# Other places for additions, scale factors, ranks and gates in the last fifth of a fused attention and FFN kernel

## The reference

```python
# block 1: a chosen 64x64 matrix per sequence, then attention with 4-bit weights
h = einsum('bct,bcd->bdt', x, cond_w[condition])
q, k, v = (h @ ((qw - 8) * scales) for each)       # 32 query heads, 8 key/value heads of 128
x = x + softmax(mask(rope(q) @ rope(k).T / sqrt(128))) @ v @ ((qw_o - 8) * scales_o)
# block 2: a gated two-layer map per sequence, then a dense layer with a routed low-rank part
h = gelu(einsum('bct,bch->bht', x * cmask, W_sess[ids]) + b_sess[ids])
s = (einsum('bht,hs->bst', h, W2) + b2) * tmask    # one row of 1024 per token
base = s @ W_base.T + b_base                       # 1024 -> 1024
logits = s @ W_router.T; top-2 of 8, softmax       # the gates w, one per token and expert
lora = 2 * einsum('ter,te,eor->to', s @ A, w, B)   # rank 16 for each of 8 experts
x = x + base + lora
```

## Time and profile before

| | us |
|---|---|
| median of three executions (lowest, highest) | 1913.29 (1912.41, 1917.9) |
| the profiled execution | 1915.91 |
| its span, first to last instruction | 1913.9 |
| busy in the span: TensorE matmul, VectorE, ScalarE, GpSimd | 1729.1, 1598.4, 1407.5, 61.3 |

### The profile page before, as it was taken

The page is one execution under the profiler, slowest core; times in us unless marked ns, Lnnn a source line. Parts: engine busy times, 40 slices in busy tenths (PEclk is TensorE's granted clock), DMA queues, the critical chain, the costliest instruction groups (busy, mean ns, idle before and its releaser), DMA issues. The chain is left out here.

```text
span 1913.9 us, 38885 instructions
## 1 busy us (share of the span) xinstructions
PE 1729.1 (90%) x14314; PEld 937.1 (49%) x14314; DVE 1598.4 (84%) x2715; ACT 1407.5 (74%) x2372; POOL 61.3 (3%) x50
## 2 busy tenths in 40 slices
PE   3668999998999899999999998999999978899998
PEld 3424545554554445445544554554544545455553
DVE  5589999999899898989998998899999987556642
ACT  2557988888898888888888888898888775233420
POOL 0200000000000000000000000000000011111100
PEclk8789999999999999999999999999999999899999
DMA  6321030011102010301021012102013111100001
GB/s 212 101 88 46 12 67 23 24 34 47 46 2 72 9 46 1 78 3 46 14 66 29 20 36 45 46 2 74 5 55 101 52 50 55 67 23 34 23 34 44
DMA packets 118582, 87.66 MB, mean 46 GB/s; under 512 B 11996, under 2 KB 110692, under 8 KB 118372
## 3 DMA queue, kind: packets, MB, share of 16 engines
q1 hardware_dynamic: 117732, 84.76, 14.9%
q10 hardware_dynamic: 640, 0.13, 0.0%
HBM read 76.49 MB, written 8.39 MB: 44 GB/s over the span
## 5 line engine op out<-in xcount | busy, mean ns | idle before, releaser
L1311 ACT ACTIVATE pj<-pj,ratio 128x512 f32<-128x512 f32 x865 | 575.4, 684 | 120.0 <-PE pj L1645 114.6
L1643 PE MATMUL pj<-hid,wts 128*128 128x512 f16 x1024 | 392.8, 384 | 66.8 <-DVE pj L826 25.0
L1645 PE MATMUL pj<-hid,wts 128*128 128x512 f16 x1024 | 390.9, 382 | 0.0
L1320 ACT ACTIVATE sbk<-sbk,wts 128x512 f32<-128x512 f32 x384 | 261.8, 682 | 24.2 <-PE sbk L1712 18.9
L1320 ACT ACTIVATE sa<-sa,wts 128x512 f32<-128x512 f32 x384 | 260.8, 679 | 15.6 <-PE sa L1712 15.5
L1643 PEld LDWEIGHTS pj<-hid,wts 128*128 128x128 f16 x1024 | 99.8, 97 | 235.8 <-ACT pj L1311 71.3
L1655 PEld LDWEIGHTS tp<-wts,hid 128*128 128x128 f16 x3072 | 181.7, 98 | 32.5 <-issue 3.5
L1655 PE MATMUL tp<-wts,hid 128*128 128x128 f16 x3072 | 192.5, 219 | 0.5
L1645 PEld LDWEIGHTS pj<-hid,wts 128*128 128x128 f16 x1024 | 100.7, 98 | 77.3 <-issue 1.4
L726 DVE SCALAR_TENSOR_TENSOR work<-pj,ratio,cos_t 128x512 f32<-128x512 f32 x128 | 95.7, 748 | 44.5 <-PE pj L1645 35.5
L1311 ACT ACTIVATE ex<-ex,ratio 128x512 f32<-128x512 f32 x193 | 127.9, 663 | 4.1 <-PE ex L1645 1.6
(11 more groups left out here) (247 smaller groups left out, 3090.4 us busy)
## 6 DMA issues: line engine op xcount, KB each, us to landing
wts<-qo_d SPq DMA_DIRECT2D x64, 256.0 KB, 3.2
y<-x_d SPq DMA_DIRECT2D x7, 2048.0 KB, 7.8
wts<-qq_d SPq DMA_DIRECT2D x35, 256.0 KB, 3.2
int_even<-qq_d SPq DMA_DIRECT2D x29, 256.0 KB, 3.0
out_d<-y SPq DMA_DIRECT2D x12, 512.0 KB, 2.6
work<-qv_d SPq DMA_DIRECT2D x16, 256.0 KB, 7.7
work<-sv_d SPq DMA_DIRECT2D x16, 256.0 KB, 9.4
work<-wb_d SPq DMA_DIRECT2D x8, 512.0 KB, 4.1
```

The source lines that it names most:

```text
L1311: act.activation(unit_bank[u][:, :], unit_bank[u][:, :], ACT.Copy, scale=ratio[:, KT * u + j:KT * u + j + 1]).then_inc(u_scaled[u], 1)
L1320: act.activation(out_bank[t % 2][:, :], out_bank[t % 2][:, :], ACT.Copy, scale=o_ratio[:, REP * t + h:REP * t + h + 1]).then_inc(o_scaled[ ...
L1643: mm(bank[:, :], w_int[:, u, j, :], hid[:, 0, j, CH * c:CH * (c + 1)], start=j == 0, stop=False, skip_group_check=True)
L1645: mm(bank[:, :], w_int[:, u, j, :], hid[:, 1, j, CH * c:CH * (c + 1)], start=False, stop=True, skip_group_check=True).then_inc(u_done[u], 1)
```

## The change

Six kinds of edit, all in the last fifth, and one at the last store. No instruction is added or taken away but one: the last tile is stored in two halves.

1. VectorE, m = 0 to 2: the first `x1_add` of a round stands before `h2_lo(m, 0)`.
2. VectorE: `chunk_factors(1)` stands before the last two `add_out` of round m = 3.
3. VectorE: `route_ranks(0)` and now `route_gates(0)` too stand before `x1_add(23)`.
4. TensorE: `turn_max(2)` stands behind `base(3)`.
5. TensorE: at i = 7, `turn(24)` stands behind `base(4)`.
6. TensorE: `turn_gates(12)` to `turn_gates(15)` stand between the two `base` halves of the tile (12 to 15) whose gates they turn; they stood behind both.
7. SyncE: the last tile is stored in two halves, each when it is ready.

```diff
@@ SyncE
-            for t in range(NT):
+            for t in range(NT - 1):
                 sp.wait_ge(S["result"], 2 * (t + 1))
                 sp.dma_start(out[P * t:P * (t + 1), :], x1_tile(t)).then_inc(S["stored"], 16)
+            for n in range(2):
+                sp.wait_ge(S["result"], 2 * (NT - 1) + n + 1)
+                sp.dma_start(out[P * (NT - 1):, 512 * n:512 * (n + 1)], x1_part(2 * (NT - 1) + n)).then_inc(S["stored"], 16)
@@ VectorE, m = 0 to 3
-                h2_lo(m, 0)
                 if turned[0]:
                     x1_add(turned[0])
+                h2_lo(m, 0)
...
                 h2_lo(m, 1)
+                if m == 3:
+                    chunk_factors(1)
...
-            chunk_factors(1)
@@ VectorE, i = 4 and 5
                 h2_lo(i, 1)
-                x1_add(k + 3)
                 if i == 5:
                     route_ranks(0)
+                    route_gates(0)
+                x1_add(k + 3)
@@ VectorE, i = 6 to 17
-                if j % CT == 0:
+                if j and j % CT == 0:
                     route_gates(j // CT)
@@ TensorE, i = 6 to 17
-                if i in (7, 8, 9, 10):
+                if i in (8, 9, 10):
                     turn(k)
                 base(2 * j + 2)
+                if i == 7:
+                    turn(k)
                 if i < NT:
                     hidden2(i, 1)
-                if i in (6, 11):
-                    turn_max(2 if i == 6 else 3)
+                if i == 11:
+                    turn_max(3)
                 route_and_lora(i - 2)
                 if i in (7, 8, 9, 10):
                     turn(k + 1)
+                if i == NT + 1:
+                    turn_gates(j + 1)
                 base(2 * j + 3)
+                if i == 6:
+                    turn_max(2)
             for j in range(NT - 4, NT):
-                turn_gates(j)
                 add_lora(2 * j)
                 add_lora(2 * j + 1)
                 if j + 1 < NT:
                     base(2 * j + 2)
+                    turn_gates(j + 1)
                     base(2 * j + 3)
```

More of the change, by code:

```diff
@@ L503, in _ @@
             load_x_again(3)
-            for t in range(NT):
+            for t in range(NT - 1):
                 sp.wait_ge(S["result"], 2 * (t + 1))
                 sp.dma_start(out[P * t:P * (t + 1), :], x1_tile(t)).then_inc(S["stored"], 16)
-            sp.wait_ge(S["stored"], 16 * NT)
+            for n in range(2):
+                sp.wait_ge(S["result"], 2 * (NT - 1) + n + 1)
+                sp.dma_start(out[P * (NT - 1):, 512 * n:512 * (n + 1)], x1_part(2 * (NT - 1) + n)).then_inc(S["stored"], 16)
+            sp.wait_ge(S["stored"], 16 * (NT + 1))
         @block.gpsimd
```

## The result

| | before | after |
|---|---|---|
| median of six executions (lowest, highest), us | 1912.85 (1910.45, 1917.9) | 1899.27 (1896.29, 1901.97) |
| the profiled execution, us | 1915.91 | 1901.97 |
| its span, us | 1913.9 | 1899.9 |
| busy: TensorE matmul, VectorE, ScalarE, us | 1729.1, 1598.4, 1407.5 | 1725.7, 1597.4, 1405.1 |

The ratio of after to before is 0.9924, with a 95% interval of [0.9912, 0.9937]: faster by 0.76%. The forecast was 1898.3 within 1894 to 1903.5. TensorE's busy time fell by 3.4 us although it does the same matmuls. The rest of the 14.0 us of span is idle time.

What follows compares the result with a forecast made beforehand. TensorE alone was taken to set the time from 1668 to 1860 us, so earlier gains reach the end. Terms 5.0 + 6.5 + 7.0 + 0.9 + 0.3 - 4.7 = 15.0 off 1913.3 gave 1898.3, range 1894 to 1903.5.

Steps and rivals of the forecast that it cites:

- Round m = 0: `turn(9)`, released by `x1_add(8)` ahead of `h2_lo(0, 0)`, starts 2.3 us earlier.
- Rounds 1 and 2: TensorE's wait moves to `turn(13)`; VectorE's two waits for ScalarE give 2.8 of 3.85 us, its chain coming 5.1 earlier.
- Round m = 3 and i = 4: `turn(17)` starts 5.7 us earlier after a new 3.4 wait; 0.7 off for the clock leaves 5.0 up to here.
- Gates of chunk 0: Ahead of `turn_gates(0)`, the 3.83 us wait and the half clock behind it go: 6.5 us won by `base(2)`.
- `turn_max(2)`: Behind `base(3)`, its 4.4 us wait and 2.6 of clock loss go: 7.0 us won.
- `turn(24)`: Behind `base(4)` it no longer waits for `chunk_factors(2)`; `turn(25)` may wait a little: 0.9 us won.
- Last gates: At `turn_gates(12)` TensorE stalls, 5.0 us plus 2.1 of clock, winning back 0.9 and 1.5: 4.7 us lost.
- Store: With half the bytes left behind the last `base_add`, the final store ends 0.3 us sooner.
- B: VectorE's chain in rounds 1 to 4 gives less, clock stays half through more: 1903.6 us, chance 14%.
- A: The stall at `turn_gates(12)` does not come: 1891.2 us, chance 6%.
- C: VectorE or a transfer paces the 192 us window, so only the stall lands: 1918.0 us, chance 3%.
- D: Moving the chunk 0 gates and `turn_max(2)` does nothing, since they wait for something else: 1911.8 us, chance 4%.

Runs made afterwards that it cites:

- with the edit alone: Kernel before with only the gates of chunk 0 moved ahead of `x1_add(23)`: 1905.53 us, ratio 0.9974 to before.
- by the edit alone: Kernel before with only `turn_max(2)` moved behind `base(3)`: 1905.68 us, ratio 0.9969 to before.
- the kernel with `turn_gates(12)` back: After kernel with `turn_gates(12)` behind `base(25)` again, turns 13 to 15 still between their halves: 1889.13 us, ratio 0.9882 to before.
- the filler: After kernel with 18 unused 512-column matmuls directly ahead of `turn_gates(12)`: 1894.09 us, ratio 0.9904 to before.

## Why the prediction was right

Every step that it named came, and each in the direction that it gave. The starts in after's trace lie 1.39 us later than in before's from ahead of the changed part on (`turn_max(0)`), so the differences of starts below are corrected by that.

- **Round m = 0**: 1549.62 to 1548.88 is, so corrected, 2.1 us, forecast 2.3 (its own numbers, 1549.62 less 1547.39, give 2.2).
- **Rounds 1 and 2**: the wait went to `turn(13)` as forecast. `x1_add(16)` moved by 1602.99 - 1599.17 + 1.4 = 5.2 us, forecast 5.1. But VectorE's two waits gave up only 3.85 - 2.46 = 1.4, where 2.8 was taken; a third, of 0.55 for a turn in round 2 (a row that I had not counted), is gone as well; and `h2_lo(m, 0)` with `x1_add` ahead takes 2.17 instead of 2.56, 0.39 less in each of two rounds. With 2.3 won by the end of round 0 that is 2.3 + 1.4 + 0.55 + 0.8 = 5.1. So the size was right and its source half wrong: the prediction had counted nothing for the 0.8. The Trainium skill, page "SBUF — State Buffer", section "Who interferes with whom", says that a VectorE instruction with two SBUF inputs contends with a GpSimd one that reads SBUF, and one with at most one SBUF input does not. The trace agrees: `h2_lo` (two SBUF inputs) took 2.56 beside the mask and 2.17 where `x1_add` (one, the other in PSUM) ran first, and in round 3, where no `x1_add` goes ahead, it is 2.55 in both kernels. No kernel without the mask was run, so the ports as the cause are not shown, only the 0.39.
- **Round m = 3 and i = 4**: `turn(17)` moved by 1604.36 - 1599.91 + 1.4 = 5.85, forecast 5.7; it waited 2.52 and not 3.4, since TensorE got there later than assumed: the `hidden2` ahead of `turn(16)`, behind a wait of 3.27 for ScalarE's rescale, took 1.89 us instead of 1.13. `base(0)` came 4.3 earlier, forecast 5.0. Here the prediction mis-sized a term: behind `turn(17)` the half clock cost 1.55 (5.85 - 4.3), not 0.7. The row of `turn(18)`, 2.07 instead of 1.16, carries most of it. The five traces with this order have heads of 68.99 to 69.58, the four with the old one 72.73 to 75.06, so the mean gain is 4.2. One trace of each would not have told it well: the old order alone spreads by 2.3.
- **Gates of chunk 0**: the stretch is 6.53 shorter (forecast 6.5), and 6.54 with the edit alone.
- **`turn_max(2)`**: 7.11 by the edit alone, forecast 7.0. **`turn(24)`**: the two stretches together are 7.96 shorter, which leaves 0.85, forecast 0.9; `turn(25)` waits 0.15.
- **Last gates**: the stall was 4.60 (forecast 4.7), the clock behind it cost 7.35 - 5.34 = 2.0 (taken 2.1), and the stretch grew by 6.35, forecast 5.0 + 2.1 - 0.9 = 6.2. What the other three tiles won back is 38.83 - 36.51 = 2.32, and 1.5 was forecast. From one tile's `add_lora` to the next it is 12.52 us instead of 13.30: beside the 0.51, a turn between two `base` halves costs 0.22 us until the next matmul starts (1864.26 to 1864.48), while ahead of `add_lora` it and its wait took 0.9. I had counted the wait alone (0.51, which the earlier trace rows show once and the trace of before four times, at 1868.07, 1881.37, 1894.68 and 1907.98). So 4.0 us were lost, forecast 4.7; the bounds of that term, 2.6 and 5.6, are 4.7 less 2.1 and plus 0.9, and the line on the range has the two signs the other way round, which changes nothing in the range.
- **Store**: the halves land sooner, and the end of the span is 0.64 closer to the last `add_lora` (4.96 to 4.32), forecast 0.3. The DMA issues after, KB each and us to landing:

```profile
out_d<-y SPq DMA_DIRECT2D x2, 256.0 KB, 2.0
```

The sum in traces is 4.3 + 6.5 + 8.0 + 0.6 - 4.0 = 15.4; less the later start of 1.4 it is the 14.0 of span. The forecast had 0.7 too much at the head and 0.7 and 0.3 too little at the last gates and the store, so the errors cancelled. The 1.4 arose ahead of the change and belongs to this pair of executions; the medians of six differ by 13.6 us and the ratio makes it 14.5. A forecast within 1 us owes some of its closeness to luck.

Of the rivals, B named the right place (the clock and VectorE's chain in the head), but lies with 1903.6 outside what was measured. A is nearly the kernel with `turn_gates(12)` back, 1889.13 where A had 1891.2; by its stretch that one instruction costs 6.4 us, forecast 6.2. C and D did not come: the 192 us window is as full as before, and edits 3 and 4 gave their gain alone.

The clock after the waits is where the prediction was only half an answer. The 4.6 us wait was followed by the lower clock, and the filler kept it at full clock. The Trainium skill, page "TensorE: Matmul & The Clock Gate", section "Part 1: The HAM clock gate (the "warmup" mystery)", says that the slow clock is the default and that activity releases it. By that rule a slow stretch behind the wait was to be expected, and the trace agrees; the size of the loss did not follow from it. These are two turns of the trace of after:

```profile
1548.88 1.16 PE L1736 MATMUL ex<-small,y 128*128 128x128 f32 x8 [3.86 <-DVE y L858]
...
1551.61 1.92 PE L1736 MATMUL ex<-small,y 128*128 128x128 f32 x8
```

And this is the first of them in another execution of the same kernel:

```profile
1545.59 2.07 PE L1736 MATMUL ex<-small,y 128*128 128x128 f32 x8 [3.86 <-DVE y L858]
```

`turn(9)` ran at 1.16 directly behind 3.86 of standing still, and what followed it up to `turn(10)` (1.92) was slow; in the other execution the same turn behind the same 3.86 took 2.07. Behind 3.27 the next 512-column matmul took 0.61 instead of 0.39 in after, and 0.39 in before. So the length of the last wait alone gives neither the start nor the size of the loss.

## What to carry to other kernels

When an engine waits for another that is itself the chain, moving an instruction ahead takes the wait away only if what it jumps goes behind every instruction that the waiting engine needs soon; three times here (`turn(13)`, `turn(17)`, `turn(18)`) the place ahead of the next such instruction gave the wait back in whole or in large part at the next turn, and a sum over the pacing engine up to the next consumer tells this beforehand. A wait that moves to a place where the waiting engine has a long independent piece to do (24 matmuls here) was gone with its lower clock as well, and the same move the other way cost both: look at each instruction of a moved group by itself, since three of the four last turns paid and one cost more than twice what they brought. Stretches between fixed instructions of one trace tell parts of 1 us apart that medians of a few executions do not.

## What the runs showed of the hardware

- The same stall of 4.60 us, the same instructions behind it: `base(25)` took 7.35, 7.20, 7.03 and 6.66 us in four executions, and 5.34 with no stall. With the wait of 3.83 for the gates in place, the stretch to `base(2)` was 32.18, 32.27, 30.96 and 30.85. What the lower clock cost behind one and the same wait differed by 0.7 and 1.4 us between executions, while stretches with no long wait in or directly ahead of them agree within 0.02 (25.64 to 25.65, 185.43 to 185.44; the 26.33 in the table has a half clock left over from a wait ahead of it).
- 18 matmuls of no use in 4.05 us ahead of the wait kept the granted clock up: 1.00 over the filler, the wait of 0.71 and `base(25)`. The row of the filler kernel from the first of them to the end of `base(25)`:

```profile
1838.10:1849.00 10.90, 10.19 (x51) 4.83 (x49) 5.29 (x14) 1.79 (x3) 0.00 (x0) 1.00 0.00 1
```

- A store of 256 KB landed in 2.0 us and one of 512 KB in 2.6: half the bytes save 0.6.
